# Turning the last batch's attention probabilities on VectorE and placing the blocks by DMA

## The reference

```
q = (hidden_states  Wq).reshape(B, Sq, H, D)
k = (encoder_hidden_states  Wk).reshape(B, Skv, H, D)
v = (encoder_hidden_states  Wv).reshape(B, Skv, H, D)
q = rmsnorm(q, gq)
k = rmsnorm(k, gk)
scores = jnp.einsum('bqhd,bkhd->bhqk', q, k) * scale
attn = jax.nn.softmax(scores, axis=-1)
out = jnp.einsum('bhqk,bkhd->bqhd', attn, v)
return out.reshape(B, Sq, H * D)  Wo
```

## Time and profile before

| | us |
|---|---|
| median of 3 runs (2068.07 to 2075.02) | 2070.37 |
| profiled execution, whole time | 2074.31 |
| profiled execution, span | 2072.5 |
| PE busy | 1919.1 |
| DVE busy | 1340.6 |
| ACT busy | 954.7 |
| POOL busy | 621.2 |

### The profile page before, as it was taken

One profiled execution on the slowest core, in us unless ns is written; L12 is line 12 of the kernel. 1 busy time (PEld: TensorE's weight loads), 2 busy tenths in 40 slices (PEclk: granted clock), 3 DMA queues, 4 the chain that ended last, 5 costly groups with the idle time before them and its releaser, 6 DMA issues.

```text
span 2072.5 us, 20300 instructions
## 1 busy us (share of the span) xinstructions
PE 1919.1 (93%) x6618; PEld 965.8 (47%) x6618; DVE 1340.6 (65%) x2016; ACT 954.7 (46%) x1852; POOL 621.2 (30%) x621
## 2 busy tenths in 40 slices
PE   7799989977998899999979999999989899997999
PEld 3355544434553345545423454454445455453543
DVE  4778875799996599978676988885752222221321
ACT  5845574544663454555525565563424235333110
POOL 1133321114652033644411354462213212221000
PEclk8789998978998799999978999999999999999999
DMA  6699952276783014787601378772111412222510
GB/s 232 206 266 257 286 163 98 87 196 150 193 198 87 12 52 121 195 227 192 160 2 41 82 198 218 173 182 62 41 41 61 158 41 88 75 71 75 199 46 35
DMA packets 148567, 272.95 MB, mean 132 GB/s; under 512 B 12648, under 2 KB 45672, under 8 KB 147440
## 3 DMA queue, kind: packets, MB, share of 16 engines
q1 hardware_dynamic: 130032, 204.55, 30.5%
q0 software_dynamic: 18432, 67.12, 16.6%
HBM read 161.91 MB, written 42.60 MB: 99 GB/s over the span
## 4 chain that ended last, share of the span: by engine, by line
PE 81%; DVE 7%; ACT 5%; DMA 3%; issue 2%; SPq 1%; POOL 0%; ACTq 0%; DVEq 0%
PE p L712 10%; PE p L690 10%; PE p L676 10%; PE p L702 9%; PE p L650 6%; PE p L749 5%; PE p L566 5%; PE p L695 5%; PE p L645 4%; PE p L657 3%; PE p L764 3%; PE p L611 2%; PE p L683 2%; PE p L547 1%; DMA s_U<-in_Wq 1%
## 5 line engine op out<-in xcount | busy, mean ns | idle before, releaser
L1010 DVE CUSTOM_DVE_ANT_0 s_U<-p,s_U 128x512 f32<-128x512 f32 x256 | 188.3, 746 | 234.5 <-PE p L690 233.5
L882 DVE TENSOR_TENSOR_SCAN s_M<-s_M 128x1024 f32<-128x1024 f32 x128 | 295.8, 2311 | 27.3 <-ACT s_M L1111 25.1
L1241 ACT COPY s_U<-p 128x512 f32<-128x512 f32 x256 | 133.7, 597 | 366.5 <-PE p L695 366.2
L676 PE MATMUL p<-s_U 128*128 128x512 f32 x512 | 268.8, 609 | 9.1 <-DMA s_U<-in_Wq 7.4
L690 PE MATMUL p<-s_U 128*128 128x512 f32 x512 | 270.8, 612 | 0.0
L1322 POOL DMA_DIRECT2D s_u<-s_M x128 | 114.0, 890 | 436.4 <-DVE s_M L887 410.5
L1366 POOL TENSOR_SCALAR s_U<-s_U 128x512 f32<-128x512 f32 x256 | 240.0, 958 | 5.9
L702 PE MATMUL p<-s_U 128*128 128x512 f32 x512 | 234.2, 600 | 4.3 <-ACT s_U L1241 2.7
L712 PE MATMUL p<-s_U 128*128 128x512 f32 x512 | 223.7, 592 | 0.7 <-issue 0.7
L1362 POOL TENSOR_TENSOR s_U<-s_U,s_mone 128x4 f32<-128x4 f32 x64 | 83.5, 1304 | 416.3 <-ACT s_U L1236 416.3
L1111 ACT ACTIVATE s_M<-s_dl,s_small 128x511 f32<-128x511 f32 x256 | 168.8, 716 | 36.7 <-DVE s_M L882 36.7
(11 more groups left out here) (172 smaller groups left out, 2526.9 us busy)
## 6 DMA issues: line engine op xcount, KB each, us to landing
s_u<-s_M POOLq DMA_DIRECT2D x128, 512.0 KB, 7.2
s_bc<-bc_scratch SPq DMA_DIRECT2D x128, 256.0 KB, 4.9
k_scratch<-s_U SPq DMA_DIRECT2D x16, 1024.0 KB, 6.9
v_scratch<-s_U SPq DMA_DIRECT2D x16, 1024.0 KB, 4.9
s_U<-in_Wq SPq DMA_DIRECT2D x64, 256.0 KB, 7.0
s_U<-k_scratch SPq DMA_DIRECT2D x64, 256.0 KB, 3.9
s_U<-v_scratch SPq DMA_DIRECT2D x64, 256.0 KB, 4.1
s_U<-in_Wo SPq DMA_DIRECT2D x64, 256.0 KB, 4.6
```

Source lines behind the costliest of these rows:

```text
L676: ins = e.matmul(banks[bk][:], wqq[j % 2][:, k, :], axT[b % 2][:, k, :], start=(k == 0), stop=(k == 3))
L882: e.tensor_tensor_scan(w, dA[i % 2], w, 0.0, ALU.mult, ALU.add).then_inc(S["m_s"], 1)
L1010: e.tensor_tensor_reduce(out=Pm[j % 2][:, k, :], in0=banks[ABANK[kind, j, k]][:], in1=rkb[j % 2], scale=rq[:, k:k + 1], scalar=-3.0e38, op ...
```

## The change

For heads 48 to 63 (`J0 = 48`) the turn leaves TensorE. After POOL's multiplication, DVE turns each tile of probabilities in blocks of 32x32 (`tr`, one instruction for 128x512) into the single buffer `turned`. Once all four tiles of a head are turned, SP issues 16 DMAs (`mv`, each 32 partitions x 512 floats, 64 KB, SBUF to SBUF) that put the blocks on their partitions in `blocks[j % 2]`. The `mix` of head j then stands in slot j+2 instead of j+1, and `w` of these heads in the slot after. ACT's four copies of turned tiles are gone for these heads; its copy of the mix puts the queries back in order. Heads 0 to 47 are as before.

```diff
+J0 = NJ - NH
 ATTN = [x for j in range(2) for x in [("q", j, k) for k in range(4)] + [("nq", j, 0)][:1 - j]]
-for j in range(NJ + 1):
+for j in range(NJ + 2):
     for t in range(4):
         ATTN += [("s", j, t)] if j < NJ else []
+        ATTN += [("tr", j - 1, t)] if J0 < j <= NJ else []
         ATTN += [("nq", j + 1, 0)] if j + 1 < NJ and t == 0 else [("q", j + 2, t - 1)] if j + 2 < NJ and t else []
-    if j > 1 and j % GH == 1:
-        ATTN += [("w", j // GH - 1, t) for t in range(4)]
-    if j:
+    if J0 < j <= NJ:
+        ATTN += [("mv", j - 1, 0)]
+    g = j // GH - 1
+    if g >= 0 and j % GH == (1 if g < J0 // GH else 2):
+        ATTN += [("w", g, t) for t in range(4)]
+    if 0 < j <= J0:
         ATTN += [("t", j - 1, t) for t in range(4)]
...
-    if j:
+    if 0 < j <= J0:
         ATTN += [("mix", j - 1, 0)]
+    elif j > J0 + 1:
+        ATTN += [("mix", j - 2, 0)]
...
+        turned = U[:, 2048:4096]
+        blocks = [U[:, o:o + 2048] for o in (13312, 0)]
...
-                        e.wait_ge(S["a_ptc"], 4 * j + 4)
+                        if j < J0:
+                            e.wait_ge(S["a_ptc"], 4 * j + 4)
+                            now = PT
+                        else:
+                            e.wait_ge(S[f"d_pt{j % 2}"], 256 * ((j - J0) // 2 + 1))
+                            now = blocks[j % 2].rearrange("p (a k q) -> p k a q", a=4, k=4)
...
+                    elif kind == "tr":
+                        e.wait_ge(S["a_pd"], 4 * j + k + 1)
+                        if k == 0 and j > J0:
+                            e.wait_ge(S[f"d_pt{(j - 1) % 2}"], 256 * ((j - 1 - J0) // 2 + 1))
+                        e.transpose(turned.rearrange("p (c k t s) -> p t k c s", c=4, k=4, t=4)[:, k],
+                                    Pm[j % 2][:, k, :].rearrange("p (k c r) -> p k c r", k=4, c=4)).then_inc(S["a_tr"], 1)
...
-                        e.copy(OT[j % NWO], banks[ABANK[kind, j, k]][:]).then_inc(S["a_oc"], 1)
+                        o, i = OT[j % NWO], banks[ABANK[kind, j, k]][:]
+                        if j >= J0:
+                            o, i = o.rearrange("p (t a s) -> p t a s", t=4, a=4), i.rearrange("p (a t s) -> p t a s", t=4, a=4)
+                        e.copy(o, i).then_inc(S["a_oc"], 1)
...
+                    elif kind == "mix" and J0 <= j < NJ - 2:
+                        e.wait_ge(S["a_o"], j + 1)
+                        load_v(j + 2)
+                    elif kind == "mv":
+                        e.wait_ge(S["a_tr"], 4 * (j - J0) + 4)
+                        e.wait_ge(S["a_o"], j if j == J0 else j - 1)
+                        for a in range(4):
+                            for c in range(4):
+                                e.dma_start(blocks[j % 2][32 * c:32 * c + 32, 512 * a:512 * a + 512],
+                                            turned[32 * a:32 * a + 32, 512 * c:512 * c + 512]).then_inc(S[f"d_pt{j % 2}"], 16)
```

More of the change, by code:

```diff
@@ L31 @@
 k_k k_v k_n k_kc k_sq k_vc k_nv k_p k_t k_tc
-a_s a_q a_nq a_pt a_o a_w a_mx a_m a_nqv a_rc a_x a_qc a_qs a_e a_ptc a_oc a_rq a_pd
+a_s a_q a_nq a_pt a_o a_w a_mx a_m a_nqv a_rc a_x a_qc a_qs a_e a_ptc a_oc a_rq a_pd a_tr
 e_xt e_g e_u e_d e_xc e_s e_rv e_rs e_hn e_it e_y
@@ L276, in context @@
         does = {"q": [("PE", 0.86)] + ([("ACT", 1.3)] if k == 3 else []), "nq": [("PE", 0.92), ("ACT", 0.3), ("POOL", 1.1)], "s": [("PE", 0.86), ("DVE", 0.9)], "ex": [("ACT", 0.95)],
-                "rc": [("POOL", 1.03 if k else 1.2)], "t": [("PE", 0.56), ("ACT", 0.6)], "mix": [("PE", 3.45), ("ACT", 0.6)], "w": [("PE", 3.45), ("DVE", 0.8)]}[kind]
-        needs = {"q": [(j // NH, "xxt", 3)] + ([] if j else [("K", KV.index((NB - 1, 3, "n", 0)))]), "nq": [(NB, "q", j, 3)], "s": [(NB, "nq", j, 0)] + ([] if j else [("K", len(KV) - 1)]) + ([(NB, "t", j - 2, 3)] if j > 1 else []), "ex": [(NB, "s", j, 3)], "rc": [(NB, "rc", j, k - 1) if k else (NB, "ex", j, 3)],
-                 "t": [(NB, "rc", j, k + 1)] + ([(NB, "mix", j - 1, 0)] if j else []), "mix": [(NB, "t", j, 3)], "w": [(NB, "mix", GH * j + GH - 1, 0)]}[kind]
+                "rc": [("POOL", 1.03 if k else 1.2)], "tr": [("DVE", 0.65)], "mv": [("DMA", 6.0)], "t": [("PE", 0.56), ("ACT", 0.6)], "mix": [("PE", 3.45), ("ACT", 0.6)], "w": [("PE", 3.45), ("DVE", 0.8)]}[kind]
+        needs = {"q": [(j // NH, "xxt", 3)] + ([] if j else [("K", KV.index((NB - 1, 3, "n", 0)))]), "nq": [(NB, "q", j, 3)], "s": [(NB, "nq", j, 0)] + ([] if j else [("K", len(KV) - 1)]) + ([(NB, "t" if j - 2 < J0 else "tr", j - 2, 3)] if j > 1 else []), "ex": [(NB, "s", j, 3)], "rc": [(NB, "rc", j, k - 1) if k else (NB, "ex", j, 3)],
+                 "t": [(NB, "rc", j, k + 1)] + ([(NB, "mix", j - 1, 0)] if j else []), "mix": [(NB, "t", j, 3) if j < J0 else (NB, "mv", j, 0)], "tr": [(NB, "rc", j, k + 1)] + ([(NB, "mv", j - 1, 0)] if j > J0 else []),
+                 "mv": [(NB, "tr", j, 3), (NB, "mix", j - 1 if j == J0 else j - 2, 0)], "w": [(NB, "mix", GH * j + GH - 1, 0)]}[kind]
         bank = [ABANK[x] for x in [(kind, j, k)] if x in ABANK]
@@ L699, in pe_attn @@
                         e.wait_ge(S[f"d_v{j % 2}"], 16 * (j // 2 + 1))
-                        e.wait_ge(S["a_ptc"], 4 * j + 4)
+                        if j < J0:
[4 more added lines that the diff above has]
+                            now = blocks[j % 2].rearrange("p (a k q) -> p k a q", a=4, k=4)
                         for kt in range(4):
-                            ins = e.matmul(banks[bk][:], V[j % 2][:, kt, :], PT[:, kt, :], start=(kt == 0), stop=(kt == 3))
+                            ins = e.matmul(banks[bk][:], V[j % 2][:, kt, :], now[:, kt], start=(kt == 0), stop=(kt == 3))
                         ins.then_inc(S["a_o"], 1)
@@ L1560, in sp_attn @@
                         load_rk(j + 2)
-                    elif kind == "s" and k == 0 and j >= 2 and j < NJ:
+                    elif kind == "s" and k == 0 and 2 <= j < J0 + 2:
                         e.wait_ge(S["a_o"], j - 1)
                         load_v(j)
+                    elif kind == "mix" and J0 <= j < NJ - 2:
[8 more added lines that the diff above has]
+                                            turned[32 * a:32 * a + 32, 512 * c:512 * c + 512]).then_inc(S[f"d_pt{j % 2}"], 16)
                     elif kind == "w" and k == 3:
```

6 lines of the change are left out of this document (4 added, 2 removed).

## The result

The change makes the kernel slower: 2092.23 us (median of 4 runs, 2086.84 to 2098.61) against 2070.34 beside it (4 runs, 2068.07 to 2075.02), a ratio of 1.0104 [1.0068, 1.014]. The prediction was 2062, with a range of 2047 to 2080. The profiled execution took 2086.84.

A forecast was written before the change was run, and what follows sets the result against it. PE was taken as the bound: 226.0 us of work, 28.3 idle (0.6 + 5.7 + 0.7 + 6.4 + 14.9) and 5.4 for clock give 259.7 against 268.3, -8.6 us; median about 2062, range 2047 to 2080.

The forecast's parts named there:

- D: Time from a head's last turn on DVE to the landing of its sixteen DMAs, put at 8.5 us.
- 15 x 0.45: SP's issue of a head's sixteen DMAs: 0.45 us each, 6.8 us to the last one.
- the transfers are slow: Rival: sixteen DMAs of 32 partitions queue up, D 10.9 to 12, +10 to +19 us, 2080 to 2089; chance 0.20.
- the 1.16 of the rival: Rival: each turn on DVE takes 1.16 us, loop 2.2 us longer, +4 us, 2075; chance 0.08.
- The loop: Single turned buffer: D, four turns and score tiles with maxima, 13.3 us a round against 11.3 of PE work.
- An output projection or a `gu` step in the slot covers it: Slots with a projection (13.7 us) or `gu` step (5.2 us) hide the 13.3 us loop; only plain slots wait.
- D's price: Each us on D costs about 7 us: three to five loops and twice at the end.
- 226.0 of work: PE's work in the stretch of heads 48 to 63: 254.3 us less 28.3 for the removed turns.
- 5.4 for the clock: Slower PE clock after idle gaps: 3.4 us at the end, 2 us from gaps in slots 60 to 62.
- The end: After the last score matmul (ends at X), two serial landings: PE idles 6.7 and 7.5 us, last landing X + 21.2.
- The stall of slot 50: PE's 8.8 us wait for the experts' fetched rows moves to slot 51 and shrinks to 5.7 us.
- Keys, scales and V: nothing: SP's other loads, behind 7 us of issues, cost nothing: keys, scales and V are used two slots later.

The follow-up runs named there:

- half: Changed kernel with each of the 16 DMAs a head copying only half of each row, 32 KB instead of 64 KB: 2080.64 us in one run.
- wide: Changed kernel with the sixteen 64 KB DMAs shaped 128 partitions by 128 floats, so no block changes partitions: 2093.42 us in one run.
- four: Changed kernel with four DMAs of 256 KB a head instead of sixteen, blocks left on the wrong partitions: 2045.36 us in one run.
- one: Changed kernel with a single 1 MB DMA a head instead of sixteen, blocks left on the wrong partitions: 2044.69 us (4 runs), ratio 0.9862.
- dpool: Changed kernel with two turned buffers and four of the sixteen DMAs a head in POOL's queue: 2047.49 us (4 runs), ratio 0.9858.
- dtail: Changed kernel with two turned buffers, heads 62 and 63 turned on TensorE, mix 61 ahead of head 62's turn: 2049.01 us (4 runs), ratio 0.9867.

## Why the prediction was wrong

**The step that failed is the issue term of D**: "15 x 0.45", and its reason, "I stay with the uncrowded rate because these DMAs bring only 64 KB each to the queue". The second to sixteenth start 0.63 us apart, so 9.4 us in place of 6.8; with the landing (2.0 for 1.6) D is 11.6, not 8.5. The bytes had nothing to do with it (`half`), nor the shape (`wide`); the number of DMAs did (`four`, `one`). All the rows that I had priced it from the earlier trace rows are loads from DRAM or stores to it; none is from SBUF to SBUF. The rate of 0.61 to 0.69 stood in my own bound, but I had laid it to a crowded queue. That is the rival "the transfers are slow" in its numbers (D of 10.9 to 12, +10 to +19 us; the stretch grew by 19.0), though not in its mechanism: the transfers were quick, the issues slow. I had given it 0.20.

The Trainium skill (DMA: Bandwidth & Descriptors, Issuing engines are not separate DMA queues) says that the issue time is usually small beside the DMA, and that several queues save only issue time. For these DMAs the first half fails: one issue takes 0.6 us and its landing 2.0, and since the transfers overlap and the issues do not, sixteen need 10.0 us of issue and only the last landing is added. The second half agrees with `dpool`, where the shorter issue was worth 9.0 us of stretch.

**The turn** takes 0.705 us, not 0.6, and not the 1.16 of the rival. The loop becomes 5.2 on DVE + 11.6 = 16.7 instead of 13.3.

**Which slots cover the loop.** "An output projection or a `gu` step in the slot covers it" held at 13.3, not at 16.7: a `gu` slot has 11.3 + 5.2 = 16.5 us of work. So there were ten waits instead of a few. I had put D's price at 7 for 1 us, and 3.1 x 7 = 22 with the -8.6 gives +13. The other 6 us of the +19 I did not split; the turn's 0.1 us, the slots that the forecast held covered and the clock are in it.

**The accounts of PE.** The forecast had 226.0 of work, 28.3 idle and 5.4 for the clock. `one`, with few gaps, is busy for 226.8, so the first term is about right. After has 44.3 idle, 16.0 more, and 243.0 - 226.0 = 17.0 us of work stretched, 11.6 more: 27.6 in all, the whole error of 287.3 against 259.7. The clock term was too small by a factor of three, since PE was idle for 4 us ahead of two of the projections, which then ran partly at the lower level, and for 11 and 8 us at the end; in `dtail`, without these gaps, a projection takes 13.9 us again. Another 4 us lie behind the stall of slot 51, for which the forecast had no clock cost at all: from 1634.03 on, the granted clock is 0.50 for 8 us, and the steps up to 1642.61 take 8.6 us instead of the 4.3 that they take in slot 55. The rows for the clock were mixed, too: besides the gap of 1.36 us in the earlier trace rows, the window of 13 us at 0.50 holds two more of the same length, so it does not show what a single such gap costs.

**The end.** By its steps: the last turn of head 62 ends at X + 3.0 (1.7 in the forecast), D, 2.5, D again: 3.0 + 11.6 + 2.5 + 11.8 = 28.9. The mechanism and the 2.5 us for four turns were right; D and the start were too small.

**The stall of slot 50** became one of 5.0 us in slot 51, forecast 5.7, but it waits for head 51's keys and not for the experts' rows, so the near hit is luck. "Keys, scales and V: nothing" was wrong there.

```profile
1623.11 0.64 SPq L1567 DMA_DIRECT2D s_U<-k_scratch  x1
...
1634.03 2.05 PE L702 MATMUL p<-s_U 128*128 128x512 f32 x2 [4.95 <-DMA s_U<-k_scratch]
```

The sixteen DMAs are not its cause: with a single one it is there too (6.5 us in `one`). SP had issued the experts' weights, 2 and 1 MB, at 1620.77 and 1621.59; the keys went out right behind them and landed after 10.8 us (median of such loads 3.8), with the DMA share at 1.0 from 1624 to 1640. So the weights are the likely cause; no run moved them. The rows came late as forecast: DVE had them normalized at 1643.2 and PE turned them at 1643.47. Without the wait for the keys, PE would have waited for the rows.

**Right**: the count of matmuls, 2.04 us less for a plain slot (13.24 to 11.20), the loop through the single buffer, DVE's wait as the thing to watch, the end as the dearest place, and "the prediction fails first where D does".

## What to carry to other kernels

Count the DMAs that a step puts in one queue and price each issue from a run of the same kind of DMA; here, with sixteen small ones a head, the queue and not the DMA engines was the bound, and fewer and larger ones or, less surely, a second queue were the cure. A single buffer between a producer and a chain of transfers closes a loop of the whole latency; a second buffer was worth 31 us here, with the same slow issues. A move that trades work for latency paid in the steady part and not at the end: leaving the last two heads on the path with the short latency took 16.5 us off the stretch.

## What the runs showed of the hardware

- An SBUF-to-SBUF DMA starts 0.63 us after the one ahead of it in SP's queue, for 32 KB as for 64 and 256 KB, and 0.52 in POOL's (2.06 for four). The DMA behind such a one takes 0.58 to 0.60 even if it is itself a load from DRAM (L1567 in after, `four` and `one`), the next ones in after and `four` 0.43 to 0.46; four loads from DRAM go out in 1.74. Why is open: I did not time SBUF-to-SBUF DMAs far apart, or stores between loads.
- 1 MB from SBUF to SBUF in one DMA lands in 5.2 us (median, `one`), 256 KB in 2.4 (`four`), 64 KB in 2.0 (after).
- DVE's 32x32 turn of 128x512 floats takes 0.705 us, 0.16 more than the pass from SBUF to SBUF of the earlier trace rows.
